# Graph layer on one core: left scores and adjacency stored later, score columns from the 16-bit halves of the turned x

## What is computed

```python
deg = max(sum(adj != 0, -1), 1)
h = relu(layernorm(x))
# layer 0
hs = h @ W_sa;  s_left = hs @ a_sa[:256];  s_right = hs @ a_sa[256:]
e = where(adj != 0, exp(-leaky_relu(s_left[:, None] + s_right[None, :], 0.01)), 0)
x_a = (e / (sum(e, 1) + 1e-5)) @ hs
x_b = adj @ (h @ W_g) + b_g
gate_a = sigmoid(concat(adj @ h, h) @ Wa.T + ba)      # gate_b with Wb, bb
x = x + sigmoid(gate_a * x_a + gate_b * x_b)
# layer 1
h = relu(layernorm(x))
x = x + relu((D^-1/2 (adj + I) D^-1/2 @ h + h) @ W1 + b1)   # D = deg
```

## Time and profile before

| | us |
|---|---|
| Median of three runs (lowest, highest) | 634.01 (633.98, 635.37) |
| The execution that was profiled | 634.38 |
| Its span in the trace | 632.5 |
| Busy: TensorE, weight loads, VectorE, ScalarE, POOL | 611.7, 525.6, 425.3, 361.8, 261.5 |

### The profile page before, as it was taken

One profiled execution on the slowest core, in us unless ns is written; L12 is line 12 of the kernel. 1 busy time (PEld: TensorE's weight loads), 2 busy tenths in 40 slices (PEclk: granted clock), 3 DMA queues, 4 the chain that ended last, 5 costly groups with the idle time before them and its releaser, 6 DMA issues.

```text
span 632.5 us, 13373 instructions
## 1 busy us (share of the span) xinstructions
PE 611.7 (97%) x5331; PEld 525.6 (83%) x5331; DVE 425.3 (67%) x811; ACT 361.8 (57%) x878; POOL 261.5 (41%) x352
## 2 busy tenths in 40 slices
PE   7989789999999999999999999999999999999997
PEld 4556557888888888888888888888888888888886
DVE  5687366799989898989898988898782122101011
ACT  3587726879878787878787878788771100000000
POOL 4438050365435252525343548223131174534433
PEclk9999979999999999999999999999999999999999
DMA  8909770897364655646465646020001085654501
GB/s 201 205 3 68 199 107 4 209 215 169 51 168 91 127 125 94 145 75 157 75 158 76 160 55 81 3 110 2 1 1 51 1 305 191 191 188 153 170 20 34
DMA packets 42073, 70.20 MB, mean 111 GB/s; under 512 B 6299, under 2 KB 34205, under 8 KB 40603
## 3 DMA queue, kind: packets, MB, share of 16 engines
q0 software_dynamic: 28544, 22.15, 25.3%
q1 hardware_dynamic: 11026, 43.01, 21.0%
q10 hardware_dynamic: 2441, 4.20, 2.1%
HBM read 69.31 MB, written 22.16 MB: 145 GB/s over the span
## 4 chain that ended last, share of the span: by engine, by line
PE 88%; DMA 4%; DVE 3%; POOL 1%; issue 1%; ACT 1%; ACTq 0%; POOLq 0%; DVEq 0%
PE accE L736 12%; PE accE L738 11%; PE accE L737 11%; PE accA L715 11%; PE accA L716 11%; PE accA L786 7%; PE accA L785 7%; PE accE L785 4%; PE accE L786 4%; DMA stage<-in_adj_dram 3%; PE tp L641 1%; PE accA L689 1%; PE accA L802 1%; PE pw L671 1%; PE pw L758 1%
## 5 line engine op out<-in xcount | busy, mean ns | idle before, releaser
L736 PE MATMUL accE<-HI,Z 128*128 128x257 f16 x676 | 184.9, 273 | 8.0 <-DVE E L1004 8.0
L738 PE MATMUL accE<-HI,E 128*128 128x257 f16 x676 | 184.6, 273 | 0.0
L737 PE MATMUL accE<-LO,Z 128*128 128x256 f16 x676 | 184.5, 273 | 0.0
L508 ACT ACTIVATE Z<-LO,sr 128x256 f32<-128x256 f32 x338 | 151.6, 498 | 40.5 <-PE accE L738 40.5
L715 PE MATMUL accA<-HI,adjT 128*128 128x260 f16 x676 | 154.0, 273 | 1.3 <-DVE adjT L990 1.3
L716 PE MATMUL accA<-LO,adjT 128*128 128x258 f16 x676 | 154.0, 273 | 0.0
L517 ACT ACTIVATE Z<-Z,sr 128x256 f32<-128x256 f32 x338 | 150.2, 497 | 0.2
L1004 DVE TENSOR_TENSOR E<-Z 128x512 bf16<-128x512 f32 x169 | 140.6, 832 | 5.8
L998 DVE TENSOR_TENSOR Z<-adjT,Z 128x512 f32<-128x512 bf16 x169 | 120.4, 712 | 18.9 <-ACT Z L517 18.7
L344 POOL DMA_DIRECT2D stage<-in_adj_dram x96 | 59.6, 657 | 100.3 <-DVE adjT L990 96.0
L786 PE MATMUL accA<-LO,adjT 128*128 128x256 f16 x416 | 91.6, 273 | 0.0
(11 more groups left out here) (123 smaller groups left out, 731.7 us busy)
## 6 DMA issues: line engine op xcount, KB each, us to landing
adjT_store<-adjT SPq DMA_DIRECT2D x11, 1664.0 KB, 6.7
stage<-in_adj_dram POOLq DMA_DIRECT2D x48, 192.0 KB, 5.0
stage<-in_adj_dram POOLq DMA_DIRECT2D x36, 224.0 KB, 8.6
adjT<-adjT_store SPq DMA_DIRECT2D x7, 896.0 KB, 4.7
adjT<-adjT_store SPq DMA_DIRECT2D x7, 768.0 KB, 5.5
stage<-adjT_store SPq DMA_DIRECT2D x4, 896.0 KB, 5.3
stage<-adjT_store SPq DMA_DIRECT2D x4, 768.0 KB, 6.1
out_dram<-late ACTq DMA_DIRECT2D x11, 256.0 KB
```

What stands on the lines that cost most here:

```text
L508: ins = act.activation(Z[:, n % RING, v], slw[:, m], ACT.Relu, bias=sr99[:, t:t + 1], scale=1.0 - SLOPE)
L736: pe.matmul(dst[:, 0:D + 1], zhi, HI[:, t, 0:D + 1], start=(t == 0), stop=False)
L737: pe.matmul(dst[:, 0:D], zhi, LO[:, t, 0:D], start=False, stop=False)
L738: ins = pe.matmul(dst[:, 0:D + 1], zlo, HI[:, t, 0:D + 1], start=False, stop=(t == TILES - 1))
```

## The change

It has five parts, all in row group 0.

- **SP** waits until both chunks of row group 1's adjacency have landed (`adj_in[1]`) before the scatter of the left scores; broadcast and store stand behind it. W1 is loaded before most of x.
- **Score columns.** The weights of the six columns are split by POOL into three bf16 parts side by side (`score_weight_parts`, 18 columns); TensorE multiplies `hTh` by all 18 and `hTl` by the first 12; VectorE sums the three parts and adds the bias. The fp32 copy `hT` is gone; `hTl` is computed from `tp` itself, and TensorE may turn the next pair when `hTl` is done.
- **Scales.** The spread is a bf16 matmul, in two lots of two, the first holding W_sa and W_g alone; the rest, W1 with it, comes in step 0.
- **Order.** Row statistics run further ahead in smaller batches, `minus_mean` moves, group 1 is turned in steps 8 and 9 instead of 7 and 8, there are fewer fillers in the loop, and the lower half of W1 comes later.
- **Finer steps.** `dense` signals each tile alone, and ScalarE copies each when it is done; the spread of pair 0's left scores goes to a bank of `accE`.

```diff
...
-    BATCHES = [(0, 1), (1, 2), (2, 4), (4, 6), (6, 8), (8, PAIRS)]
+    BATCHES = [(0, 1), (1, 2), (2, 3), (3, 4), (4, 5), (5, 7), (7, 9), (9, PAIRS)]
...
-        hT = sb("hT", [P, 2, HALVES, 2 * P])
...
         w6 = sb("w6", [P, 6, HALVES])
+        w6rest = sb("w6rest", [P, 6, HALVES])
+        w6s = sb("w6s", [P, HALVES, 18], BF16)
+        scored = sb("scored", [P, 2, 6])
...
-        wdiag = ub[:].rearrange("p e d -> p (e d)").rearrange("p (k n) -> p k n", k=4)
+        wdiag = ub[:].rearrange("p e d -> p (e d)").bitcast(BF16)[:, 0:4 * P].rearrange("p (k n) -> p k n", k=4)
+        ones16 = ones[:].bitcast(BF16).rearrange("p (n w) -> p n w", w=2)[:, :, 1]
...
             sp.dma_start(wsg[0], W_sa.rearrange("(h p) o -> p h o", p=P)).then_inc(wsg_in, 16)
             for k, w in enumerate((ba, bb)):
                 sp.dma_start(bias6[:, 1 + k:2 + k], bass.AP(w.tensor, 0, [[0, P], [1, 1]])).then_inc(bias_in, 16)
+            sp.dma_start(w1, W1.rearrange("(h p) o -> p h o", p=P)).then_inc(w1_in, 16)
...
-            sp.dma_start(w1, W1.rearrange("(h p) o -> p h o", p=P)).then_inc(w1_in, 16)
...
+
+            sp.wait_ge(adj_in[1], adj_count(1, 1))
             spread_left(0)
             keep_adj(0)
             spread_left(1)
...
-                pool.wait_ge(winv_ok, 1)
+                pool.wait_ge(winv_ok, 2)
...
+            def score_weight_parts():
+                pool.wait_ge(wprep, 2 * HALVES)
+                pool.wait_ge(w6_ok, 2)
+                part = [w6s[:, :, 6 * j:6 * j + 6].rearrange("p h k -> p k h") for j in range(3)]
+                pool.tensor_copy(part[0], w6[:]).then_inc(w6s_ok, 1)
+                pool.wait_ge(w6s_ok, 1)
+                pool.tensor_tensor(w6rest[:], w6[:], part[0], ALU.subtract).then_inc(w6r_ok, 1)
+                pool.wait_ge(w6r_ok, 1)
+                pool.tensor_copy(part[1], w6rest[:]).then_inc(w6s_ok, 1)
+                pool.wait_ge(w6s_ok, 2)
+                pool.tensor_tensor(part[2], w6rest[:], part[1], ALU.subtract).then_inc(w6s_ok, 1)
...
             load_adj(0, 0)
             inv_stds(2)
+            score_weight_parts()
             load_adj(0, 1)
             loads = {4: (1, 0), 5: (1, 1), 9: (2, 0), 10: (2, 1)}
             for s in range(PAIRS):
                 score_parts(s)
-                if s in (0, 1, 4):
-                    inv_stds({0: 3, 1: 4, 4: 5}[s])
+                if s == 0:
+                    inv_stds(3)
+                if s in (0, 1, 2, 4):
+                    inv_stds({0: 4, 1: 5, 2: 6, 4: 7}[s])
                 gate_columns(s)
                 if s in loads:
                     load_adj(*loads[s])
...
-                    act.wait_ge(dn_ps, i - 1)
+                    act.wait_ge(dn_ps, 2 * i - 2)
                 act.activation(hTh[:, i % 2].rearrange("p h n -> p (h n)"), tp[:], ACT.Copy).then_inc(hTh_ok, 1)
-                act.activation(hT[:, i % 2].rearrange("p h n -> p (h n)"), tp[:], ACT.Copy).then_inc(hT_ok, 1)
...
-                act.wait_ge(dn_ps, i + 1)
                 src = dn[:].rearrange("p (e k d) -> p e k d", e=2, k=2)
                 for e in range(2):
+                    act.wait_ge(dn_ps, 2 * i + e + 1)
...
-                act.activation(slw[:, 0], pw[:, 256:512], ACT.Copy).then_inc(left_ok, 1)
+                act.activation(slw[:, 0], bank(accE, 1)[:, 0:2 * P], ACT.Copy).then_inc(left_ok, 1)
...
+                if s == 0:
+                    first_halves(0)
                 if s + 1 < PAIRS:
                     turned(s + 1)
                 if s + 2 < PAIRS:
                     norm(s + 2)
                 if 0 <= s - 4 < PAIRS:
                     expo(0, s - 4)
-                if s < PAIRS:
+                if 0 < s < PAIRS:
                     first_halves(s)
-                if s == 0:
+                if s == 1:
                     left_first()
                 if 0 <= s - 3 < PAIRS:
                     leaky(0, s - 3)
-                if s == 5:
+                if s == 9:
...
                 pe.wait_ge(hf_ok, 2 * i + 2)
                 if i >= 1:
-                    pe.wait_ge(hT_ok, i)
+                    pe.wait_ge(hTl_ok, i)
                 transposes(tp, hf[:, i % 2]).then_inc(hT_ps, 1)
...
-                    pe.wait_ge(wprep, 2 * HALVES)
-                    pe.wait_ge(w6_ok, 2)
-                pe.wait_ge(hT_ok, i + 1)
+                    pe.wait_ge(w6s_ok, 3)
+                pe.wait_ge(hTl_ok, i + 1)
                 if i >= 1:
                     pe.wait_ge(srw_ok, i)
-                if i == 1:
-                    pe.wait_ge(left_ok, 1)
                 for e in range(2):
                     for h in range(HALVES):
-                        ins = pe.matmul(pw[:, 6 * e:6 * e + 6], hT[:, i % 2, h, e * P:(e + 1) * P], w6[:, :, h],
-                                        start=(h == 0), stop=(h == HALVES - 1))
+                        rows = slice(e * P, (e + 1) * P)
+                        pe.matmul(pw[:, 18 * e:18 * e + 18], hTh[:, i % 2, h, rows], w6s[:, h], start=(h == 0),
+                                  stop=False)
+                        ins = pe.matmul(pw[:, 18 * e:18 * e + 12], hTl[:, i % 2, h, rows], w6s[:, h, 0:12],
+                                        start=False, stop=(h == HALVES - 1))
                 ins.then_inc(proj, 1)
...
-                pe.matmul(pw[:, 256:512], ones[:], diag[:].rearrange("p e n -> p (e n)"), start=True,
+                pe.matmul(bank(accE, 1)[:, 0:2 * P], ones[:], diag[:].rearrange("p e n -> p (e n)"), start=True,
...
-                ins.then_inc(dn_ps, 1)
+                    ins.then_inc(dn_ps, 1)
...
-                pe.matmul(accE[:, 0:(k1 - k0) * P], ones[:], wdiag[:, k0:k1].rearrange("p k n -> p (k n)"),
+                pe.matmul(accE[:, 0:(k1 - k0) * P], ones16, wdiag[:, k0:k1].rearrange("p k n -> p (k n)"),
...
+                    pe.wait_ge(left_ok, 1)
...
             keep_busy(8)
-            spread_weights(0, 3, 1)
-            keep_busy(4)
             turn(0)
-            keep_busy(16)
+            spread_weights(0, 2, 1)
+            keep_busy(20)
             for s in range(PAIRS):
                 dense(s)
                 if s == 0:
+                    turn(1)
                     project(0)
-                    turn(1)
+                    spread_weights(2, 4, 2)
                     keep_busy(4)
+                if s == 1:
                     widen_first()
                 if s + 2 < PAIRS:
                     turn(s + 2)
-                if s < 4:
-                    keep_busy(6)
-                if s == 4:
-                    spread_weights(3, 4, 2)
+                if 1 <= s < 4:
+                    keep_busy(4)
...
-                dve.wait_ge(hT_ok, i + 1)
-                dve.tensor_tensor(hTl[:, i % 2], hT[:, i % 2], hTh[:, i % 2], ALU.subtract).then_inc(hTl_ok, 1)
+                dve.tensor_tensor(hTl[:, i % 2].rearrange("p h n -> p (h n)"), tp[:],
+                                  hTh[:, i % 2].rearrange("p h n -> p (h n)"), ALU.subtract).then_inc(hTl_ok, 1)
...
-                taken = pw[:, 0:12].rearrange("p (e k) -> p e k", k=6)
-                dve.tensor_tensor(srw[:, 2 * i:2 * i + 2, :], taken,
+                dve.tensor_reduce(out=scored[:], in_=pw[:, 0:36].rearrange("p (e j k) -> p e k j", e=2, j=3),
+                                  axis=mybir.AxisListType.X, op=ALU.add).then_inc(scored_ok, 1)
+                dve.wait_ge(scored_ok, i + 1)
+                dve.tensor_tensor(srw[:, 2 * i:2 * i + 2, :], scored[:],
...
             row_stats(0)
+            row_stats(1)
+            dve.wait_ge(wsg_in, 32)
+            largest(0, 1)
+            minus_mean(0)
+            largest(1, 2)
+            on_diagonal(0, 2)
+            minus_mean(1)
             gate_weights()
-            dve.wait_ge(wsg_in, 32)
-            largest(0, 2)
-            minus_mean(0)
-            largest(2, 3)
-            on_diagonal(0, 3)
-            row_stats(1)
-            scales(0, 3, 1)
-            minus_mean(1)
-            row_stats(2)
-            row_stats(3)
+            scales(0, 2, 1)
+            dve.wait_ge(w1_in, 16)
+            largest(2, 4)
             turned_second(0)
             second_weights(0)
             second_weights(1)
+            row_stats(2)
             score_weights()
             minus_mean(2)
-            turns = {3: (0, 0), 4: (0, 1), 7: (1, 0), 8: (1, 1)}
-            for s in range(PAIRS + 4):
+            on_diagonal(2, 4)
+            second_halves(0)
+            take_scores(0)
+            turned_second(1)
+            row_stats(3)
+            diagonal_first()
+            scales(2, 4, 2)
+            row_stats(4)
+            minus_mean(3)
+            turns = {3: (0, 0), 4: (0, 1), 8: (1, 0), 9: (1, 1)}
+            for s in range(1, PAIRS + 4):
                 if s < PAIRS:
                     take_scores(s)
-                if s == 0:
-                    diagonal_first()
                 if s + 1 < PAIRS:
```

(24 more changed lines are left out.)

## The result

The changed kernel takes **619.21 us** (median of 4 runs, 619.04 to 621.8) where the kernel before takes 634.27 beside it (4 runs, 633.98 to 635.37): a ratio of 0.977, 95% interval 0.974 to 0.980. The forecast was 620.5, with a range of 617 to 626. The execution profiled took 619.04 us, 15.34 less than the 634.38 against which the sum was made.

What follows compares the result with a forecast made beforehand. TensorE was taken to bound the kernel from 120 us on, with VectorE pacing steps 1 to 4 of row group 0. 634.4 - 1.8 - 10.4 - 1.9 = 620.3, with small waits 620.5 us; range 617 to 626.

Steps and rivals of the forecast that it cites:

- The accident: TensorE's 6.83 us idle before 81.50 and slow clock after, behind row group 1's late load; SP's wait removes it: -10.4 us.
- the scatter's path: SP's scatter of the left scores, after its new wait, runs from 59 to 70.3 us; the wait costs nothing.
- The score matmuls: TensorE, steps 6 to 12: eight 16-bit matmuls take 0.50 us instead of 0.81, saving 0.31 a step, 1.9 us.
- The rival built on 98 ns a load: Narrow score matmuls bound by weight loads: 0.78 us a step, 2 us more, 622.5 us; chance 0.16.
- The head: Start of the kernel: dense(0) at 14.0 us against 16.19, turned_second(1) done at 19.3 in place of 22.1.
- VectorE paces to step 5: Steps 1 to 4: VectorE's 24.3 us of work and 3.1 of waits put dense(6) at 50.7 us, -1.8 us.
- The sum: Whole kernel: 634.4 - 1.8 - 10.4 - 1.9 = 620.3, with small waits 620.5 us; chance 0.55.
- The sum for the lower end: Load-free score matmuls (1.8 us less) and a VectorE chain without 3.1 us of waits reach 616.5; set at 617.
- Accident moved: Rival: row group 1 lands late anyway, or the scatter slows group 2's load: 10 us back, 630.5 us; chance 0.07.
- Slower than before: Rival: the clock falls before turn(2) at 18.7 us and stays low while every step has a gap: 640 us; chance 0.04.
- Clock falls in a new gap: Rival: TensorE's clock falls in a gap of steps 2, 4 or 5, costing 3.5 us: 624 us; chance 0.15.
- The prediction's own sign of being wrong: A stage-1 idle of TensorE, or a clock row below 1 between 20 and 60 us, would make the forecast wrong.

Runs made afterwards that it cites:

- a3: The kernel before with only row group 1's turns moved one step later, to steps 8 and 9, without SP's wait: 625.18 us.
- a1: The changed kernel without SP's wait before the scatter of the left scores: 619.87 us.
- a2: The kernel before with SP's wait before the scatter alone added: 624.15 us.
- after_again: The changed kernel unchanged, run again as base of a later set: 619.51 us.
- b2: b1 with the row statistics of pairs 11 and 12 moved from VectorE's step 4 to steps 5 and 6: 617.55 us.
- c2: The changed kernel with three unused VectorE additions (some 1.9 us) in step 7, where nothing is turned: 619.63 us.
- d1: b2 with mean products of batches 4 to 6 earlier, minus_mean(8) before step 8's second halves, third weight matrix's halves in step 11: 614.41 us.
- b1: The changed kernel with VectorE subtracting the next step's turned x ahead of the adjacency turns in steps 3 and 4: 617.95 us.
- c1: The changed kernel with three unused VectorE additions (some 1.9 us) ahead of the turns of step 4: 622.48 us.

## Why the prediction was right, and which term was off

*The accident, -10.4.* Right in size (10.38), and right that the late piece is slowed by what SP moves beside it: without that it lands in 6.3 us. The prediction named the scatter alone, where 13 of the 21.2 us lie beside the broadcast and the store; which of the three is to blame no run shows. And it gave all of it to SP's wait, and mentioned the turns' new steps in one closing sentence as a margin. a3 shows that the margin alone was enough, by 0.35 us, and a1 that without the wait the changed kernel is no slower. The step "the wait takes the accident away" is shown by a2; in the change itself the later turns would have done it in these runs, and the wait adds reserve. The forecast of the scatter's path held: issued 59.78 (59), landed 71.10 (70.3).

*The score matmuls, -1.9, is the mis-sized term.* They were put at 0.50 us a step, between bounds of 0.48 and 0.78 that both rested on a recorded load of 98 ns or a part of it. Measured is 0.20. The recorded loads still read 96 ns, but they overlap one another; here three loads of the score matmuls, stationary operands of 128 columns, and the mean of eight:

```profile
50.88 0.10 PEld L694 LDWEIGHTS pw<-w6s,hTl 128*128 128x128 f16 x1
50.90 0.10 PEld L692 LDWEIGHTS pw<-w6s,hTh 128*128 128x128 f16 x1
50.93 0.10 PEld L694 LDWEIGHTS pw<-w6s,hTl 128*128 128x128 f16 x1
```

```profile
L692 PEld LDWEIGHTS pw<-w6s,hTh 128*128 128x128 f16 x8 | 0.6, 96 | 0.0
```

A load starts 25 ns after the one before and lasts 96 in the record. A row's duration was taken for the spacing, and here that is not what limits the rate. The rule of the Trainium skill, "TensorE: Matmul & The Clock Gate", section on LDWEIGHTS, of P / 1.2 ns for P columns, 107 ns here, is near the recorded 96 ns of one load. Read as the distance from one load to the next, as the prediction did for its rival, it would have made these eight 0.86 us and the step no shorter; the run disagrees with that reading, with eight loads of 128 columns in 0.20 us. The rival built on 98 ns a load falls with it. The term becomes 0.61 a step, 3.7 over six steps; of it 3.2 arrived. The remainder went in steps 9 and 10, which took 5.66 and 5.69 us instead of 5.43, where the turns of TensorE started 0.42 and 0.45 us after the last dense matmul, not 0.22: at 70.15 and 75.84 us, just behind VectorE's subtractions from 69.32 and 75.01 (0.68 each), themselves behind the adjacency's turns in steps 8 and 9.

*The head.* dense(0) came at 14.55 against 14.0 forecast, VectorE's turned_second(1) ended at 19.50 against 19.3. The inverse scales were there at 11.06, as forecast (11.05). Then VectorE stood 0.76 us, to 11.82, until W1's load had landed, 8.7 us after its issue, and behind that wait in its queue are turned_second(0) and the weight halves for which dense(0) waits. The prediction put this term at nothing, with up to 1 us if it delayed other rows; W1's own lateness is what it left out, and it is more than the whole 0.55. The same wait is 1.01 us in after_again, 0.32 in b2 and 0.25 in c2. In the other profiled executions with this head it is W_g's load that VectorE waited for (0.33 to 1.54 us, in b2 as well), save in d1, which waited for neither and started dense(0) at 13.74.

*VectorE paces to step 5.* The strongest part. The sum of what VectorE owes, 24.3 and 3.1 of waits, was to end the split of unit 0 at 46.6; it ended at 47.03, 27.5 us after 19.50 against 27.4 forecast, its waits 0.78, 1.69 and 0.48 us against 0.7, 1.7 and 0.7. The gaps of 1.65, 2.35 and 2.8 us were 1.76, 2.32 and 3.00. dense(6) came at 51.08 against 50.7, so -1.4 in place of -1.8. b1, c1 and c2 confirm the pacing from both sides: less ahead of the subtraction gives 1.8 us, 1.9 more costs all of it and a fall of the clock, and the same 1.9 in step 7 costs under 0.5 in the trace.

*The sum.* -1.41 - 10.38 - 3.16 and 0.39 around it against -1.8 - 10.4 - 1.9: two errors of opposite sign, 0.4 and 1.3, and 0.4 that no term foresaw. The last cancels the first, which is luck; the 1.3 us by which the result lies under the forecast are the mis-sized term. The sum for the lower end does not come out either: 620.5 less 1.8 and 3.1 is 615.6, not the 616.5 given, though the 617 chosen held.

*The rivals.* Accident moved: refuted, the pieces of row group 2 landed in 10 to 14 us beside the broadcast and the store and nothing waited for them. Slower than before: refuted by the time; the clock row of the first profiled execution reads 9 throughout. Clock falls in a new gap: the mechanism is real, the price was wrong. The prediction's own sign of being wrong, a clock row below 1 between 20 and 60 us, did not occur in the first profiled execution; it did in that of after_again, the same kernel, whose stretches are these:

```profile
32.00:34.00 2.00, 2.00 (x6) 0.69 (x5) 1.90 (x11) 0.47 (x1) 0.44 (x2) 0.50 0.01 2
34.00:36.00 2.00, 2.00 (x12) 1.14 (x11) 1.21 (x3) 1.55 (x4) 1.85 (x7) 0.84 0.00 0
...
42.00:44.00 2.00, 2.00 (x11) 1.48 (x10) 1.97 (x7) 1.38 (x3) 0.00 (x0) 0.50 0.03 8
```

Two falls to 0.50, and yet from dense(0) to dense(6) it takes 36.99 us instead of 36.53: 0.5 us, not 3.5 each. In a1's profiled execution, with both falls, it takes 36.91; in c2's, with the second alone, 37.04. In steps 1 to 5 the slower TensorE fills a gap in which it would have waited for VectorE: before the turn of step 5 it waits 1.43 us in after_again and 3.00 in the first execution. So a fall did not by itself make the forecast wrong; the sign was too strict. The 3.5 was the price of a fall in which all lost time lay on the path and which lasted 6.9 us, from 81.50 to about 88.4 by the starts of the matmuls. c1's lay on the path too, lasted some 3.5 us and cost 1.67: in both, half of the time at the lower level.

## What to carry to other kernels

When a transfer lands late, ask of each remedy separately whether it removes the lateness or only the waiting for it; one of two that come in one edit may be redundant, and a kernel of each alone tells. A remedy that only gives more room holds as long as the lateness stays inside it. The cost of a short pipelined instruction is read from the distance between the starts of its neighbours and not from the duration in its row (here 25 ns against 96 and 170); without such neighbours in the trace the lower bound must go well under that duration. Where two engines take turns in pacing, a saving on the one that waits is worth nothing there, and an edit that moves work out of the pacing stretch must also ask which small product at the end of a queue becomes late (here the late place of a 0.16 us operation, with the weight halves moved beside it, cost 1.5).

## Hardware behaviour not expected

- 16-bit matmuls of 18 and 12 columns, each with its own load of 128 columns, start 25 ns apart at full clock (0.20 us for eight, in the changed kernel). The fp32 ones of 6 columns took 0.101 us a pass in the kernel before.
- The clock fell in some executions and not in others of the same kernel. In after_again and a1 it read 0.50 in 32 to 34 and 42 to 44 us, in b2 in the first of the two alone and in c2 in the second alone, behind gaps (1.76 and 2.31 us) that the first profiled execution of the changed kernel had as well (1.76 and 2.32) without any fall; that one also came through a gap of 3.00 us at full clock, while behind 4.89 us in c1 it read 0.56. Which gap is too long is not settled by these runs.
- A scatter of 6 KB in elements of four bytes takes 11.2 to 13.7 us to land. The last piece of row group 1 (224 KB), issued beside it and with the broadcast and the store behind it, lands in 15.6 to 21.2 us, and in 6.3 or 6.4 where SP's three transfers wait for it. Beside the broadcast and the store, row group 2's first pieces take 11.8 us instead of 4.3. What they share was not tried.
